# A Mamba block between two routed feed-forwards on one core: the next unit's transposes stand one third of a product sooner in TensorE's order

## The chip, the core and the metric

The kernel runs on one NeuronCore of a Trainium2 chip. The metric is the device time of one execution in microseconds. Before the change three runs took 2841.54, 2841.79 and 2851.29 us; the median is 2841.79 us.

## What is computed

4096 tokens (2 sequences of 2048) of 1024 features go through three residual stages:

```python
x = x + 0.5 * _L0_ffn_ref(_layernorm(x), A, B, W, bias)
x = x + _L0_attn_ref(_layernorm(x), W_xproj, W_dt, b_dt, A_log, D_param)
x = x + 0.5 * _L0_ffn_ref(_layernorm(x), A, B, W, bias)
```

The feed-forward projects each row on 64 experts of rank 16, keeps the four with the largest norm, and adds their low-rank update to a dense product:

```python
vecs = jnp.einsum('arh,bsh->bsar', A, x)
_, idx = jax.lax.top_k(jnp.linalg.norm(vecs, axis=-1), 4)
routes = jax.nn.one_hot(idx, 64).sum(-2) / 4
v = jnp.einsum('bsa,bsar->bsr', routes, vecs)
delta = jnp.einsum('bsa,ajr,bsr->bsj', routes, B, v)
base = jnp.einsum('bsh,jh->bsj', x, W) + bias
```

The middle stage is a selective scan with 16 states per feature: from a small projection come delta (a softplus), B and C; each state follows h = exp(delta A) h + delta B x, and y is the sum over the states of h C, plus x D.

## The kernel before, in words

**Units.** The 4096 tokens are 32 blocks of 128 rows. A block passes the first feed-forward as a unit of kind 1 and the second as a unit of kind 2, so there are 64 units, in an order that `plan` sets. The program of each engine is written out by hand as one `unit(l, a, b)` per unit: a is the present unit, l the one before, b the next. TensorE works on the base and routed products of a and, at the end, on the expert products of b.

**The scan** is cut into 256 groups of four (128 x 512) tiles. Each group is multiplied by B on POOL (`times_b`), decayed by exponentials on ACT (`decay`, line 855), scanned on DVE (line 1062), multiplied by C on POOL (`times_c`, line 459) and summed over the states on TensorE (`states`, line 651: four instructions, which the trace shows as eight). The groups are spread over units 5 to 57, four or five to a unit. The deltas come from a product on TensorE (`z`, line 638), a softplus on ACT (lines 814 to 829) and a product on DVE; they are written to delta_scratch and read back, broadcast over the states, by SP's queue.

**From a's choice to b's experts**, which is the part around the change. DVE sums the squares of the expert products (line 1010) and picks the four largest (`choose`), gathers the chosen vector and writes it to sel (`gather`), and SP's queue transposes it into uT. TensorE meanwhile runs a's base product (xT by wW), then a's routed product (uT by wB). Each product is made in two halves of 512 columns (nb 0 and 1) and each half in three thirds of eight matmuls 128x512: high part of the rows by high and low weights, k 0 to 3 (third 0) and k 4 to 7 (third 1), both line 491, and the low part of the rows by the high weights (third 2, line 495).

DVE takes the statistics of b's rows (`unit_stats`), ACT refines the inverse deviation in small steps (lines 740 to 754) and writes the normalised rows to xn (`normed`, line 764). TensorE transposes xn in eight 128x128 blocks (`norm_blocks`, line 483): the first four into pv, the other four into pt. The first call waits for xn:

```python
def norm_blocks(b, half):
    if half == 0:
        pe.wait_ge(s_xn, b.u + 1)
    if half == 0:
        pe.wait_ge(s_u, b.u * 2)
```

ACT copies each half to the high part of xT (`high`, line 769), DVE subtracts that to make the low part (`low_part`, line 1006). On both engines these two steps stand among decays and scans in a fixed order. After both high copies and the first low one TensorE may start the 48 matmuls of b's experts (`experts`, xT by wA into pv); its third third waits for the second low part. ACT squares the result (`squares`, line 777), and the next choice begins. In units of kind 1 ACT normalises a's rows a second time for the scan (`normed2`, line 787), ahead of the second call of `squares`.

All four engines and SP's queue execute in order. A wait holds back everything behind it on its engine, and semaphores are the only ties between engines.

Of the kernel before, what the change touches and what calls it, by code (L numbers as in the profile page):

```python
# [78 lines left out]
def build(nc, x, AT, BT, WT, bias, WxT, WdtT, b_dt, A_log, D_par, out):  # L79
# [38 lines left out]
    with ctx:  # L118
# [359 lines left out]
        def _(pe):  # L478
            pe.wait_ge(s_id, 3)

            def blocks(dst, src, sem_done, idt):
                for k in range(KB):
                    last = nc.tensor.transpose(dst[:, k * P:(k + 1) * P], src(k), idt)
                last.then_inc(sem_done, 1)

            def product(dst, lhs, w, nb, third, first, stop):

                if third < 2:
                    for k in range(third * KB, (third + 1) * KB):
                        for wb in range(2):  # L490
                            last = nc.tensor.matmul(dst, lhs[:, 0, k, :], w[:, wb, k, nb * HF:(nb + 1) * HF],  # L491
                                                    start=(first and k == 0 and wb == 0), stop=False)
                else:
                    for k in range(KD):
                        last = nc.tensor.matmul(dst, lhs[:, 1, k, :], w[:, 0, k, nb * HF:(nb + 1) * HF],  # L495
                                                start=False, stop=(stop and k == KD - 1))
                return last
# [6 lines that stand above are left out]
                blocks(ptn[half], lambda k: xn[:, (half * KB + k) * P:(half * KB + k + 1) * P], s_xT, idf[:, :])  # L504

            def y_blocks(b, half):
                if half == 0:
                    pe.wait_ge(s_ldy, b.v * 16 + 16)
                else:
                    pe.wait_ge(s_u, b.u * 2)  # L510
                blocks(pty[half], lambda k: auxy[:, half * KB + k, :], s_yT, idf[:, :])
# [50 lines left out]
            def base(a, nb, third):  # L562
                if a.u == 0:
                    if nb == 0 and third == 0:
                        first_base(a)
                    return
                if third == 0:
                    pe.wait_ge(s_res, max(a.u * 2 - 1 + nb, 0))
                    nc.tensor.matmul(po[:, nb, :], onesb[:, :], brow[:, nb * HF:(nb + 1) * HF], start=True, stop=False)
                product(po[:, nb, :], xT, wW, nb, third, False, False)  # L570

            def first_routed(a):

                pe.wait_ge(s_uc[0], 16)
                pe.wait_ge(s_uc[1], 16)
                for k in range(KD):
                    pe.wait_ge(s_hiB, k + 1)
                    for part in range(2):
                        for nb in range(2):
                            nc.tensor.matmul(po[:, nb, :], uT[:, part, k, :], wB[:, 0, k, nb * HF:(nb + 1) * HF],  # L580
                                             start=False, stop=False)
                for k in range(KD):
                    if k < KB:
                        pe.wait_ge(s_loB, k + 1)
                    else:
                        pe.wait_ge(s_loBp, k + 1 - KB)
                    for nb in range(2):
                        last = nc.tensor.matmul(po[:, nb, :], uT[:, 0, k, :], wB[:, 1, k, nb * HF:(nb + 1) * HF],
                                                start=False, stop=(k == KD - 1))
                        if k == KD - 1:  # L590
                            last.then_inc(s_out, 1)

            def routed(a, nb, third):
                if a.u == 0:
                    if nb == 0 and third == 0:
                        first_routed(a)
                    return
                if nb == 0 and third != 1:
                    pe.wait_ge(s_uc[third // 2], 16 * a.u + 16)
                last = product(po[:, nb, :], uT, wB, nb, third, False, True)  # L600
                if third == 2:
                    last.then_inc(s_out, 1)

            def scan_blocks(l, half):
                if half == 0:
                    pe.wait_ge(s_xn2, l.w + 1)
                else:
                    pe.wait_ge(s_nc, l.w * 2 + 1)
                blocks(pt, lambda k: xn[:, (half * KB + k) * P:(half * KB + k + 1) * P], s_nT, idf[:, :])
# [13 lines left out]
            def turn_products(l):  # L623

                pe.wait_ge(s_pk, l.w + 1)
                nc.tensor.transpose(pj[:, 2 * P:3 * P], pjs[:, 0:P], idf[:, :])
                nc.tensor.transpose(pj[0:NX - P, 3 * P:4 * P], pjs[:, P:NX], idf[:, :]).then_inc(s_pq, 1)

            def z(a, pos):
                if pos not in a.zs:  # L630
                    return
                t = a.zs[pos]
                q, k = t // KD, t % KD
                if k == 0:
                    pe.wait_ge(s_ldr, 16 * (q + 1))
                pe.wait_ge(s_gm, a.u + 1)
                pe.wait_ge(s_dc, t)
                nc.tensor.matmul(pz, wdt[:, k * P:(k + 1) * P], drT, start=True, stop=True).then_inc(s_z, 1)

            def states(a, n):  # L640

                G = slot_of(a, n)
                if G is None or G < 2 or G - 2 >= NGRP:
                    return
                G -= 2
                g = G % 4
                pe.wait_ge(s_cm, G + 1)
                if g == 0:
                    pe.wait_ge(s_y, G // 4)
                for s in range(4):  # L650
                    last = nc.tensor.matmul(py[32 * s:32 * s + 32, :], Em[:, :], Hr[:, G % NH, s, :],  # L651
                                            start=(g == 0), stop=(g == 3), tile_position=(0, 32 * s))
                last.then_inc(s_e, 1)

            def unit(l, a, b):
                late = l if l and l.kind == 1 else None
                y = b if b and b.kind == 2 else None
                base(a, 0, 0)
                if late:
                    scan_blocks(late, 0)  # L660
                base(a, 0, 1)
                states(a, 0)
                base(a, 0, 2)
                if late:
                    scan_blocks(late, 1)
                z(a, 0)
                base(a, 1, 0)
                if y:
                    if late:
                        pe.wait_ge(s_nc, late.w * 2 + 2)  # L670
                    y_blocks(y, 0)
                if y:
                    y_blocks(y, 1)
                base(a, 1, 1)
                base(a, 1, 2)
                states(a, 1)
                if late:
                    scan_products(a, late, y)
                if late:
                    pe.wait_ge(s_nc, late.w * 2 + 2)  # L680
                if y:
                    pe.wait_ge(s_ya, y.v * 2 + 2)
                routed(a, 0, 0)
                if late:
                    turn_products(late)
                routed(a, 0, 1)
                if late:
                    pe.wait_ge(s_pc, late.w + 1)
                routed(a, 0, 2)
                states(a, 2)  # L690
                routed(a, 1, 0)
                z(a, 1)
                routed(a, 1, 1)
                if b:
                    norm_blocks(b, 0)
                if b:
                    norm_blocks(b, 1)
                routed(a, 1, 2)
                states(a, 3)
                z(a, 2)  # L700
                if b:
                    experts(b, 0, 0)
                if b:
                    experts(b, 0, 1)
                if b:
                    experts(b, 0, 2)
                if b:
                    pe.wait_ge(s_dc, a.z_end)
                    experts(b, 1, 0)
                if b:  # L710
                    experts(b, 1, 1)
                if b:
                    experts(b, 1, 2)
                states(a, 4)
# [4 lines left out]
            for l, a in zip([None] + US, US):  # L719
                unit(l, a, a.after)  # L720
# [491 lines left out]
```

## Time and profile before

| | |
|---|---|
| median of the runs | 2841.79 us (2841.54 to 2851.29) |
| profiled execution: span | 2851.0 us |
| the run it is taken to be | 2851.29 us, the highest of the three |
| PE busy | 2604.9 us, 91% |
| POOL busy | 2347.1 us, 82% |
| DVE busy | 2189.6 us, 77% |
| ACT busy | 1448.4 us, 51% |
| PE weight loads | 1158.5 us, 41% |

The span is the time from the first to the last instruction of one profiled execution. A busy share is an average over the whole span: POOL works only while the scan runs, from about 300 to 2640 us, so its share there is much higher than the 82%. In rows of the trace "L483" is line 483 of the kernel; PE is TensorE, PEld its weight loads. A number in square brackets in a row is the idle time of the engine just before, with what ended it.

### The profile page before, as it was taken

The page shows a single profiled execution, that of the slowest core. Times are in us where ns is not written, and L with a number is a line of the kernel's source. Part 1 is how long each engine was busy: PE and PEld are TensorE (multiplying, and loading weights), DVE is VectorE, ACT ScalarE, POOL GpSimd, SP SyncE. Part 2 cuts the span into 40 slices and gives each one's busy share as a digit, 9 for nine tenths or more (in the row PEclk, how much of TensorE's full clock was granted, in tenths as well). Part 3 has the DMA queues.
Part 4 walks back from the last instruction along what each step waited for, and adds up shares of the span by engine and source line. Part 5 has one row for each costly group of instructions (what it writes and reads, how often), then busy time and mean ns, then how long its engine had stood idle before and what let it go on. Part 6 is the DMA issues. An engine that isn't in the chain of part 4 may idle for free.

```text
span 2851.0 us, 38123 instructions
## 1 busy us (share of the span) xinstructions
PE 2604.9 (91%) x13056; PEld 1158.5 (41%) x13120; DVE 2189.6 (77%) x2661; ACT 1448.4 (51%) x3075; POOL 2347.1 (82%) x703
## 2 busy tenths in 40 slices
PE   4998999999899999989999999999899989988999
PEld 1454444444333434334444343444334433433444
DVE  7434788788888878888888788888888888878533
ACT  5334565555555555545655465555555545454211
POOL 2103999899999999999899999999999999999300
PEclk8999999999999999999999999999999999999999
DMA  5125445554445444554454346444454455444221
GB/s 214 51 62 132 140 133 137 155 154 141 127 131 159 129 129 139 154 137 134 130 167 133 116 131 169 144 127 141 148 148 144 118 157 148 123 137 122 67 60 52
DMA packets 309368, 373.40 MB, mean 131 GB/s; under 512 B 148147, under 2 KB 224051, under 8 KB 309174
## 3 DMA queue, kind: packets, MB, share of 16 engines
q1 hardware_dynamic: 292278, 337.40, 40.7%
q10 hardware_dynamic: 16896, 33.56, 4.0%
q8 instruction: 104, 1.70, 0.2%
q14 instruction: 90, 0.74, 0.1%
HBM read 234.05 MB, written 103.29 MB: 118 GB/s over the span
## 4 chain that ended last, share of the span: by engine, by line
PE 22%; DVE 18%; POOL 10%; DMA 8%; issue 7%; DVEq 5%; ACT 4%; ACTq 1%; SPq 1%; POOLq 0%
DVE mreg L1062 9%; PE pv L491 7%; POOL mreg L459 5%; PE po L491 5%; PE pv L495 3%; POOL mreg L451 3%; DMA delta_scratch<-mreg 3%; PE po L495 3%; DMA mreg<-xnT_scratch 2%; PE py L651 2%; ACT pA L855 1%; POOL mreg L446 1%; DMA uT<-sel 1%; DVE pv L1029 1%; DVE sel L1026 1%
## 5 line engine op out<-in xcount | busy, mean ns | idle before, releaser
L459 POOL TENSOR_TENSOR mreg<-mreg 128x2048 f32<-128x2048 f32 x256 | 1161.1, 4536 | 20.9 <-ACT hst L844 20.7
L1062 DVE TENSOR_TENSOR_SCAN mreg<-pA,hst,mreg 128x512 f32<-128x512 f32 x768 | 940.1, 1267 | 75.5 <-ACT hst L844 45.5
L451 POOL TENSOR_TENSOR mreg<-mreg 128x1024 f32<-128x1024 f32 x340 | 795.8, 2365 | 234.9 <-DMA mreg<-delta_scratch 231.9
L855 ACT ACTIVATE pA<-mreg,nA 128x512 f32<-128x512 f32 x1024 | 696.7, 684 | 467.2 <-DVE mreg L1062 412.9
L491 PE MATMUL po<-wB,uT 128*128 128x512 f16 x2016 | 476.7, 386 | 30.3 <-DMA uT<-sel 16.9
L491 PE MATMUL pv<-wA,xT 128*128 128x512 f16 x2016 | 462.4, 383 | 39.6 <-ACT xT L769 30.5
L491 PE MATMUL po<-wW,xT 128*128 128x512 f16 x2016 | 467.0, 380 | 8.0 <-issue 7.0
L446 POOL TENSOR_TENSOR mreg<-mreg 128x2048 f32<-128x2048 f32 x86 | 390.7, 4544 | 1.6 <-issue 1.6
L1062 DVE TENSOR_TENSOR_SCAN mreg<-pA,cst,mreg 128x512 f32<-128x512 f32 x256 | 313.4, 1267 | 30.4 <-ACT hst L844 20.7
L491 PEld LDWEIGHTS pv<-wA,xT 128*128 128x128 f16 x2016 | 194.0, 99 | 320.6 <-ACT xT L769 76.6
L491 PEld LDWEIGHTS po<-wB,uT 128*128 128x128 f16 x2016 | 192.7, 99 | 321.9 <-issue 94.2
L651 PE MATMUL py<-mreg,Em 128*32 128x512 f32 x2048 | 272.9, 605 | 50.2 <-POOL mreg L459 40.7
L491 PEld LDWEIGHTS po<-wW,xT 128*128 128x128 f16 x2016 | 197.6, 98 | 225.6 <-issue 13.7
L1010 DVE TENSOR_REDUCE n<-sel 128x32 f32<-128x512 f32 x128 | 86.6, 677 | 250.0 <-ACT sel L777 249.9
L495 PE MATMUL pv<-wA,xT 128*128 128x512 f16 x1008 | 243.2, 385 | 27.0 <-DVE xT L1006 27.0
L495 PE MATMUL po<-wB,uT 128*128 128x512 f16 x1008 | 243.2, 385 | 0.0
L495 PE MATMUL po<-wW,xT 128*128 128x512 f16 x1008 | 240.1, 381 | 0.0
L495 PEld LDWEIGHTS pv<-wA,xT 128*128 128x128 f16 x1008 | 98.6, 99 | 150.9 <-issue 36.4
L1042 DVE SCALAR_TENSOR_TENSOR xin<-po,sc,xin 128x512 f32<-128x512 f32 x128 | 92.2, 721 | 85.8 <-PE po L495 82.4
L495 PEld LDWEIGHTS po<-wW,xT 128*128 128x128 f16 x1008 | 94.5, 98 | 151.6 <-issue 45.7
L777 ACT ACTIVATE sel<-pv 128x512 f32<-128x512 f32 x128 | 75.4, 590 | 152.5 <-PE pv L495 148.0
L495 PEld LDWEIGHTS po<-wB,uT 128*128 128x128 f16 x1008 | 100.2, 99 | 108.6 <-issue 6.0
(132 smaller groups left out, 2346.9 us busy)
## 6 DMA issues: line engine op xcount, KB each, us to landing
mreg<-delta_scratch SPq DMA_DIRECT2D x256, 512.0 KB, 5.6
delta_scratch<-mreg ACTq DMA_DIRECT2D x128, 256.0 KB
xin<-x SPq DMA_DIRECT2D x32, 512.0 KB, 4.5
x_scratch<-xin SPq DMA_DIRECT2D x32, 512.0 KB, 7.2
xnT_scratch<-auxs SPq DMA_DIRECT2D x32, 512.0 KB, 2.9
mreg<-xnT_scratch SPq DMA_DIRECT2D x64, 256.0 KB, 6.4
mreg<-bc_scratch SPq DMA_DIRECT2D x64, 256.0 KB, 5.5
yT_scratch<-mreg SPq DMA_DIRECT2D x64, 256.0 KB, 2.4
```

The lines of the kernel that those rows point to most:

```text
L446: pool.tensor_tensor(Hr[:, G % NH, :, :], u, b.broadcast_to([P, 4, CT]), ALU.mult).then_inc(s_bm, 2)
L451: pool.tensor_tensor(Hr[:, G % NH, 2 * h:2 * h + 2, :], u, b.broadcast_to([P, 2, CT]), ALU.mult).then_inc(s_bm, 1)
L459: pool.tensor_tensor(h, h, Cr[:, g, :].unsqueeze(1).broadcast_to([P, 4, CT]), ALU.mult).then_inc(s_cm, 1)
L491: last = nc.tensor.matmul(dst, lhs[:, 0, k, :], w[:, wb, k, nb * HF:(nb + 1) * HF], start=(first and k == 0 and wb == 0), stop=False)
L495: last = nc.tensor.matmul(dst, lhs[:, 1, k, :], w[:, 0, k, nb * HF:(nb + 1) * HF], start=False, stop=(stop and k == KD - 1))
L651: last = nc.tensor.matmul(py[32 * s:32 * s + 32, :], Em[:, :], Hr[:, G % NH, s, :], start=(g == 0), stop=(g == 3), tile_position=(0, 32 * s))
L777: nc.scalar.activation(sel[:, nb * HF:(nb + 1) * HF], pv[:, nb, :], ACT.Square).then_inc(s_sq, 1)
L855: nc.scalar.activation(pA[:, i % 2, :], Dr[:, 2 * (n % NPR) + i % 2, :], ACT.Exp, scale=nA[:, c:c + 1]).then_inc(s_dA, 1)
L1010: V.tensor_reduce(n2[:, nb * NE // 2:(nb + 1) * NE // 2], sel3[:, nb * NE // 2:(nb + 1) * NE // 2, :], AX.X, ALU.add)
L1026: V.tensor_tensor(ranked, pv[:, :, :].rearrange("p b (a r) -> p r (b a)", r=R16), mask[:, :].unsqueeze(1).broadcast_to([P, R16, NE]), ALU. ...
L1042: V.scalar_tensor_tensor(dst, po[:, nb, :], sc[:, 3:4], dst, ALU.mult, ALU.add).then_inc(s_res, 1)
L1062: V.tensor_tensor_scan(h, pA[:, i % 2, :], h, before, ALU.mult, ALU.add).then_inc(s_sc, 1)
```

## The change

In TensorE's `unit`, the two calls of `norm_blocks` for the next unit move ahead of the call `routed(a, 1, 1)`. The eight matmuls of that call now stand behind the transposes, together with the eight of `routed(a, 1, 2)`.

```diff
@@ -690,11 +690,11 @@
                 states(a, 2)
                 routed(a, 1, 0)
                 z(a, 1)
+                if b:
+                    norm_blocks(b, 0)
+                if b:
+                    norm_blocks(b, 1)
                 routed(a, 1, 1)
-                if b:
-                    norm_blocks(b, 0)
-                if b:
-                    norm_blocks(b, 1)
                 routed(a, 1, 2)
                 states(a, 3)
                 z(a, 2)
```

TensorE's order in a scan unit, from the state products `states(a, 2)` (py) over the second half of the routed product (po<-wB,uT) and the transposes (pv and pt from idf,xn) to the expert products (pv<-wA,xT); before:

```order
L651 MATMUL py<-mreg,Em 32x512 x4
L491 MATMUL po<-wB,uT 128x512 x16
L483 MATMUL pv<-idf,xn 128x128 x4
L483 MATMUL pt<-idf,xn 128x128 x4
L495 MATMUL po<-wB,uT 128x512 x8
L651 MATMUL py<-mreg,Em 32x512 x4
L491 MATMUL pv<-wA,xT 128x512 x16
```

The same place after the change:

```order
L651 MATMUL py<-mreg,Em 32x512 x4
L491 MATMUL po<-wB,uT 128x512 x8
L483 MATMUL pv<-idf,xn 128x128 x4
L483 MATMUL pt<-idf,xn 128x128 x4
L491 MATMUL po<-wB,uT 128x512 x8
L495 MATMUL po<-wB,uT 128x512 x8
L651 MATMUL py<-mreg,Em 32x512 x4
L491 MATMUL pv<-wA,xT 128x512 x16
```

The sixteen matmuls of line 491 are split: eight stand ahead of the transposes as before, eight behind. The other engines' orders and the DMA queues are unchanged, as is the first unit, whose routed product is written in another form.

## Rows read from the trace of the kernel before

**Rows 1.** Busy time by stretch: us, then each engine's busy time (instructions).

```profile
core 0: us, PE busy (x) PEld busy (x) DVE busy (x) ACT busy (x) POOL busy (x), PEclk, DMA share, GB/s
700.00:2640.00 1940.00, 1780.25 (x8980) 773.50 (x9022) 1608.76 (x1902) 1049.51 (x2200) 1876.51 (x552) 0.98 0.48 139
2700.00:2851.00 151.00, 145.94 (x696) 68.69 (x697) 50.77 (x84) 23.25 (x60) 0.00 (x0) 1.00 0.20 56
```

**Rows 2.** Waits from 300 to 2640 us: engine line <- releaser: us, times, longest.

```profile
DVE n L1010 <- ACT sel L777: 151.3, 60, 4.5
...
POOL mreg L451 <- DMA mreg<-delta_scratch: 52.5, 21, 6.4
...
PE pv L491 <- ACT xT L769: 29.2, 23, 3.1
PE pv L483 <- ACT xn L764: 27.9, 23, 2.7
```

**Rows 3.** Chain that ended last, its first piece: start us, us, what.

```profile
709.71 0.04 issue
```

**Rows 4.** The same chain, pieces around the experts' start in three units.

```profile
1060.99 0.70 DVE xT L1006
...
1332.33 0.52 ACT xT L769
...
1332.88 0.70 DVE xT L1006
...
1333.72 3.61 PE pv L491 x16
...
1344.28 0.61 ACT sel L777
...
2374.67 0.70 DVE xT L1006
```

**Rows 5.** The same chain, the eight matmuls ahead of the transposes.

```profile
1465.16 1.73 PE po L491 x8
```

**Rows 6.** Timeline of unit 60: start us, us, engine, line, operation.

```profile
2703.84 1.24 ACT L764 ACTIVATE xn<-xin,ln_nm,ln_r 128x1024 f32<-128x1024 f32 x1
...
2711.05 0.60 PE L483 MATMUL pv<-idf,xn 128*128 128x128 f32 x4
```

**Rows 7.** Timeline around 1465 us.

```profile
1464.63 1.24 ACT L764 ACTIVATE xn<-xin,ln_nm,ln_r 128x1024 f32<-128x1024 f32 x1
...
1466.72 0.60 PE L483 MATMUL pv<-idf,xn 128*128 128x128 f32 x4
```

**Rows 8.** Timeline around 1330 us.

```profile
1328.31 1.24 ACT L764 ACTIVATE xn<-xin,ln_nm,ln_r 128x1024 f32<-128x1024 f32 x1
...
1329.61 0.66 PE L483 MATMUL pv<-idf,xn 128*128 128x128 f32 x4 [0.63 <-ACT xn L764]
...
1330.54 1.89 PE L495 MATMUL po<-wB,uT 128*128 128x512 f16 x8
...
1332.36 1.06 PE L651 MATMUL py<-mreg,Em 128*32 128x512 f32 x8
...
1333.72 1.46 PE L491 MATMUL pv<-wA,xT 128*128 128x512 f16 x6 [0.29 <-DVE xT L1006]
```

**Rows 9.** The chain again, pieces of the passages from xn to the matmuls.

```profile
1368.90 1.25 ACT xn L764
...
1371.64 3.06 PE po L495 x8
...
2594.94 1.25 ACT xn L764
```

**Rows 10.** Timeline around 875 us.

```profile
874.45 1.24 ACT L764 ACTIVATE xn<-xin,ln_nm,ln_r 128x1024 f32<-128x1024 f32 x1
...
876.20 0.60 PE L483 MATMUL pv<-idf,xn 128*128 128x128 f32 x4
```

**Rows 11.** Timeline of TensorE at 1370 us.

```profile
1370.20 0.66 PE L483 MATMUL pv<-idf,xn 128*128 128x128 f32 x4 [2.37 <-ACT xn L764]
```

**Rows 12.** Busy time by stretch, 1368 to 1376 us (PEclk follows POOL).

```profile
1368.00:1376.00 8.00, 5.80 (x26) 2.57 (x27) 7.03 (x9) 6.07 (x12) 8.00 (x4) 0.79 0.55 167
```

More of the change, by code:

```diff
@@ L692, in unit @@
                 z(a, 1)
-                routed(a, 1, 1)
                 if b:
@@ L697, in unit @@
                     norm_blocks(b, 1)
+                routed(a, 1, 1)
                 routed(a, 1, 2)
```

## The prediction, made before the changed kernel was run

> **What bounds the kernel now.** I read the time by stretches first. In the scan stretch from 700 to 2640 us POOL works 1876.5 of 1940 us (97%), TensorE 1780.3 (92%) and DVE 1608.8 (83%); in the last 151 us POOL does nothing and TensorE works 145.9 us [rows 1]. So the ends are TensorE's alone, and in the middle three engines are close to each other. The table of waits says that none of them is a bound that hides the others. POOL stops 21 times for rows that come back from delta_scratch, 52.5 us in all. DVE stops 60 times for the squares of the expert products, 151.3 us. TensorE stops 23 times for the normalised rows (27.9 us) and 23 times for the ACT copies of xT (29.2 us) [rows 2]. The last two waits are the ones on either side of what the change moves.
>
> Then I read the chain of waits, since in such a balance it alone says what a microsecond is worth. It reaches back to 709.71 us [rows 3] and no further; of what lies ahead of that I have only the other views. It changes engines many times in each unit. The piece at 1332 us shows the part that matters: DVE makes the low half of xT, TensorE runs the 48 expert products after it, ACT squares them from 1344.28 us [rows 4], DVE sums and chooses, and only then come the scans of the next unit. When the experts start late there, all that follows is late.
>
> **What the change does at one passage.** The eight matmuls that change places with the transposes take 1.73 us [rows 5]. Nothing is added or removed: the matmuls and the transposes are the same, no DMA is issued sooner or later by its own queue, and ACT, DVE, POOL and SP keep their order. So the direct cost is nothing, and all depends on when the rows (xn) are ready. Three cases occur in the trace.
>
> (a) TensorE comes late. In the last units xn begins at 2703.84 us and takes 1.24, and the transposes run at 2711.05, 5.97 us after its end [rows 6]. They go 1.73 us sooner, TensorE waits for nothing before or after, and the sum stays: 0. The units ahead of the scans are of this kind too.
>
> (b) TensorE comes a little late. At 1464.63 + 1.24 = 1465.87 us the rows are ready and the transposes start at 1466.72 [rows 7], 0.85 later. They can go only 0.80 us sooner (about 0.05 passes between the end of xn and the first transpose where TensorE waits for it [rows 8]), so what stands behind is 1.73 - 0.80 = 0.93 us later. In ten or so units of this kind the experts start later than TensorE is free, by 0.9 us or more, since ACT's second copy stands behind a softplus. The 0.93 is taken up there, and I cost it at 0; if ACT were ready, it would cost 0.93 each.
>
> (c) TensorE comes first. At 1328.31 us xn begins; TensorE has waited 0.63 us when it transposes at 1329.61; eight matmuls follow at 1330.54, the eight state products at 1332.36, then 0.29 us of waiting, and the experts start at 1333.72 [rows 8]. Now TensorE waits for xn 1.73 us longer, the transposes start when they did, and sixteen matmuls stand behind them. It is ready for the experts 1.73 us later than before, 0.29 of which was a wait for xT. The experts start 1.73 - 0.29 = 1.44 us later. The added cover hides nothing that was open beyond these 0.29 us.
>
> By the timeline some 30 of the 53 scan units are of kind (c), but only those on the chain count. In several units of the first feed-forward, whose rows are normalised a second time, the chain goes through ACT's and DVE's own work, and the experts have time to spare. **The passages on the chain** are these:
> - low half of xT to experts: six times, the first at 1060.99 us and the last at 2374.67 [rows 4], each with the same wait of 0.29 or 0.30 before the experts: 6 x 1.44 = 8.6 us.
> - xn to transposes to matmuls to experts without a further wait: three times, the first at 1368.90 us and the last at 2594.94 [rows 9]: 3 x 1.73 = 5.2 us.
> - at 876.20 us TensorE comes 0.51 us after the end of xn (874.45 + 1.24) [rows 10] and there is no wait before the experts: 1.73 - 0.46 = 1.3 us.
> - the passage at 1466.72 us [rows 7], where POOL takes over from the state products behind the eight matmuls: 0.9 us.
>
> The sum is 16.0 us for 1931 us of scan units on the chain (709.7 to 2640). The scan units ahead of it, from about 300 to 710 us, show the same kinds of passage; an estimate in proportion is 16.0 x 410 / 1931 = 3.4 us. In all **+19.4 us**. The profiled execution has a span of 2851.0 us and lies at 2851.29 us, the highest of the three runs (their median is 2841.79). 2851.3 + 19.4 = 2870.7, a ratio of 1.0068, and on the median 2861.1: I forecast **2861 us**.
>
> The bounds. Below: the chain has near ties that I can't see, other executions are up to 10 us shorter and may follow another chain, and POOL's 97% may take up part of it: 0. Above: every one of 53 units late by 1.73 is 92 us, less the 29.2 us of waiting before the experts [rows 2], 63 us. I stay near the sum, since it is counted passage by passage on a chain without slack and nothing on that chain gets shorter.
>
> **The clock.** At the passage of 1368.90 us TensorE waited 2.37 us for xn [rows 11], and in the 8 us from 1368 the granted clock is 0.79 [rows 12], so a part ran at 1.2 GHz instead of 2.4. From the first transpose (1370.20) to the end of the eight matmuls (1371.64 + 3.06) it took 4.50 us [rows 9, 11], against 2.75 at full clock (1329.61 to 1332.36) [rows 8]: 1.75 us more. The change lengthens the wait ahead of the transposes by up to 1.73 us in kind (c) and shortens the one behind. I leave this out of the sum, since most waits of kind (c) become about 2 us long, shorter than the one of rows 11, and no row says what such a wait does. The Trainium skill (TensorE: Matmul & The Clock Gate, section "Why this matters for your kernels") advises against idle gaps between bursts of matmuls, because the clock falls to half; by that rule more passages would start at half clock after the change, and the sum would be that of rival 2, below.
>
> **Rivals.**
> 1. *POOL hides it.* POOL is busy 97% of the scan stretch, and the eight-matmul delays fall into DVE's and TensorE's slack while POOL goes on. The time stays at 2842. The Trainium skill (Perfetto Trace Analysis, section "Identifying the Most-Contended Engine") has the engine of highest occupancy as the one to optimise; read strictly, a delay on TensorE would then not count. Against it: POOL stops 21 times for the delta rows [rows 2], which come from a chain that starts with TensorE in the same unit. Chance 0.23.
> 2. *Half clock.* By the timeline 8 further passages of kind (c) get a wait about as long as that of rows 11 or longer; if each begins at half clock, at 1.75 us, that is 14 us on top, 2875 us. For it speaks the one clear case [rows 11, 12]. Against it: equally long waits just before the experts become shorter. Chance 0.20.
> 3. *Faster.* If the copies to xT were held by the transposes, transposing sooner would start the experts sooner and remove their waits for xT: at most 29.2 us [rows 2], 2841.8 - 29.2 = 2813 us. It decides in kinds (a) and (b), wherever the first copy starts at the end of the transposes. In kind (c) the transposes can't go sooner. And even where they can, in scan units ACT is busy with decays: the copy at 1332.33 [rows 4] began 2 us after its four transposes, which had started at 1329.61 and taken 0.66 [rows 8]. Chance 0.07.
>
> **How the numbers follow.** My own case has 0.50 and spans 2848 to 2872. A measurement of this kernel can tell about 0.5% from no change, which is 14.2 us: slower begins at 2856. Some of my own case (0.08) lies under it, so slower is 0.42 + 0.20 = 0.62, plus 0.01 from late switches of the chain: 0.63. Within 0.5%: 0.23 + 0.08 = 0.31, less that 0.01 and with 0.01 of the third rival: 0.31. Faster 0.06. The range from 2843 to 2880 leaves out the third rival, about half of the first and the upper tail.
>
> **What would show it.** In the changed profile TensorE's wait for xn (23 times, 27.9 us) should grow to 60 to 90 us over 30 units or more, its wait for the xT copies should fall from 29.2 to under 15, and in kind (c) the experts should start 5.6 us after the end of xn instead of 4.2. DVE's wait for the squares should grow by 10 to 40 us, and POOL's busy time in the scan stretch should stay while the stretch gets longer. I am wrong if the wait for xn grows but POOL's idle time does not, or if the copies to xT start sooner and the experts with them.

## The result, and the profile after

| | before | after |
|---|---|---|
| median of the runs | 2845.3 us (2841.54 to 2851.29) | 2883.95 us (2881.77 to 2886.15) |
| profiled execution, span | 2851.0 us | 2881.9 us |
| PE busy | 2604.9 us | 2622.8 us |
| POOL busy | 2347.1 us | 2346.8 us |
| share of PE in the chain that ended last | 22% | 27% |

A further run of the kernel before moved its median from 2841.79 to 2845.3 us. Its profiled execution is the slowest of its runs, so the two spans are only 31 us apart. The ratio is **1.0131**, with a 95% interval from 1.0119 to 1.0143: the change costs about 37 us. The forecast had the sign and the places right, but 19.4 us and a range that ended at 2880.

The waits from 300 to 2670 us, the same scan units as in [rows 2] (engine, line, releaser: us in total, times, longest):

```profile
DVE n L1010 <- ACT sel L777: 170.5, 60, 5.6
PE pv L483 <- ACT xn L764: 106.1, 50, 4.4
...
POOL mreg L451 <- DMA mreg<-delta_scratch: 69.6, 22, 6.7
...
PE pv L491 <- ACT xT L769: 3.8, 8, 1.0
```

TensorE's wait for the normalised rows grew from 27.9 to 106.1 us and from 23 to 50 times. Its wait for xT went from 29.2 to 3.8 us. DVE waits 19 us longer for the squares, and POOL 17 us longer for the delta rows. The other waits of POOL over the same units, first before, then after:

```profile
POOL mreg L459 <- ACT hst L844: 19.1, 8, 3.2
POOL mreg L451 <- PE py L651: 3.0, 4, 1.5
POOL mreg L446 <- issue: 1.6, 2, 1.4
```

```profile
POOL mreg L459 <- ACT hst L844: 20.4, 8, 3.3
POOL mreg L446 <- issue: 8.2, 5, 2.3
POOL mreg L451 <- PE py L651: 8.2, 5, 3.4
```

With the delta rows that is 76.2 us before and 106.4 after. POOL's work is the same (2347.1 and 2346.8 us), so its 30 us more of waiting are the 31 us between the two spans. The late experts reach the time as idle time of POOL, 17 us of it at the delta rows.

Busy time by stretch (columns as in [rows 1]), the scan units and the end:

```profile
700.00:2670.00 1970.00, 1796.96 (x8970) 780.63 (x9012) 1609.27 (x1900) 1048.68 (x2201) 1875.53 (x551) 0.97 0.47 136
2730.00:2881.00 151.00, 146.93 (x702) 69.26 (x703) 51.67 (x85) 23.23 (x60) 0.00 (x0) 1.00 0.20 56
```

Against [rows 1] the scan stretch takes 30 us more for the same work of POOL (1875.5 us and 1876.5), and the end is unchanged. The granted clock of the scan stretch is 0.97 instead of 0.98.

The chain that ended last, at the passage that answers to [rows 8]:

```profile
1331.87 1.25 ACT xn L764
...
1333.17 0.66 PE pv L483 x4
1333.82 0.44 PE pt L483 x4
1334.26 1.73 PE po L491 x8
1335.98 1.73 PE po L495 x8
1337.71 1.00 PE py L651 x8
1338.71 3.56 PE pv L491 x16
...
1349.21 0.61 ACT sel L777
```

This is kind (c) as the prediction drew it. The rows end at 1333.12 us, the transposes follow at once, then sixteen matmuls and the state products, and the experts start at 1338.71 without a wait: 5.6 us after the end of xn instead of 4.2. The chain now runs from xn through TensorE. In the traced part of before, from 709.7 us, it did so three times; after, in a traced part that is shorter (from 1011.1 us), it does so 23 times, 19 of them in the 26 units that the experiments single out below, and four in others. The first and the last:

```profile
1054.57 1.25 ACT xn L764
...
2667.52 1.25 ACT xn L764
```

The next passage shows the other part of the loss. The timeline of TensorE, and the busy time with the granted clock (third number from the end):

```profile
1375.13 1.11 PE L483 MATMUL pv<-idf,xn 128*128 128x128 f32 x4 [4.09 <-ACT xn L764]
...
1376.89 3.58 PE L491 MATMUL po<-wB,uT 128*128 128x512 f16 x8
...
1382.13 1.06 PE L651 MATMUL py<-mreg,Em 128*32 128x512 f32 x8
1383.12 1.25 PE L491 MATMUL pv<-wA,xT 128*128 128x512 f16 x5
```

```profile
1374.00:1382.00 8.00, 6.87 (x24) 3.60 (x24) 7.05 (x9) 5.33 (x9) 8.00 (x4) 0.61 0.64 208
```

The same passage of before waited 2.37 us [rows 11] at a clock of 0.79 [rows 12]. Now TensorE waits 4.09 us and then works at 1.2 GHz for longer: the granted clock over 8 us is 0.61, the first eight matmuls take 3.58 us, against 1.89 for eight at full clock [rows 8], and the experts start 8.0 us after the end of xn. By the clock records of the traces TensorE was at the lower level for 68 us (17 stretches) between 280 and 2700 us before, and for 109 us (26 stretches) after.

### The profile page after: what moved, and what is told of

Same layout as the page of the kernel before. It is cut to its first block, busy times and chain, and to the rows that moved or that the text cites. A ratio compares the mean times of both kernels' runs of the same rounds, so it can differ in the third digit from the quotient of the medians.

```text
span 2881.9 us, 38123 instructions
## 1 busy us (share of the span) xinstructions
PE 2622.8 (91%) x13056; PEld 1165.8 (40%) x13120; DVE 2191.3 (76%) x2661; ACT 1447.6 (50%) x3075; POOL 2346.8 (81%) x703
## 4 chain that ended last, share of the span: by engine, by line
PE 27%; DVE 12%; DMA 7%; POOL 4%; issue 4%; DVEq 4%; ACT 4%; SPq 1%; ACTq 1%; POOLq 0%
PE pv L491 7%; PE po L491 7%; DVE mreg L1062 6%; PE pv L495 4%; PE po L495 4%; DMA delta_scratch<-mreg 2%; DMA xin<-x_scratch 2%; PE py L651 2%; DMA mreg<-xnT_scratch 2%; POOL mreg L459 2%; POOL mreg L451 2%; DVEq L984 1%; ACT xn L764 1%; PE pv L620 1%; POOL mreg L446 1%
## 5 line engine op out<-in xcount | busy, mean ns | idle before, releaser
L491 PE MATMUL po<-wB,uT 128*128 128x512 f16 x2016 | 498.3, 395 | 25.8 <-DVE xin L992 15.3
L491 PEld LDWEIGHTS po<-wB,uT 128*128 128x128 f16 x2016 | 197.0, 101 | 305.3 <-issue 94.7
L495 PE MATMUL po<-wB,uT 128*128 128x512 f16 x1008 | 239.6, 381 | 0.0
L483 PE MATMUL pv<-idf,xn 128*128 128x128 f32 x256 | 45.7, 306 | 117.3 <-ACT xn L764 117.3
```

## The experiments

Theory W: the cost comes from the wait for the normalised rows, which stands eight matmuls sooner, in the units where TensorE comes first; it holds back what follows and lets the clock fall. The change itself is the first row of this table, and the two columns on the right are worked out from each kernel's own trace: the mean time from the end of xn to the first expert matmul over the 26 scan units without a delta product at position 1 (`1 not in a.zs`), and the time at the lower clock from 280 to 2700 us.

| kernel | ratio to before (95%) | experts after xn | lower clock |
|---|---|---|---|
| the change | 1.0131 (1.0119 to 1.0143) | 6.28 us | 109 us |
| before | 1 | 4.51 | 68 |
| e1 wait alone | 1.0117 (1.0099 to 1.0134) | 6.31 | 116 |
| e2 units with a delta product | 0.9991 (0.9982 to 1.0001) | 4.51 | 51 |
| e3 units without | 1.0130 (1.0110 to 1.0150) | 6.20 | 99 |
| e4 change and 8 filling matmuls | 1.0082 (1.0064 to 1.0100) | 5.67 | 82 |
| e5 before and 4 filling matmuls | 0.9999 (0.9989 to 1.0008) | 4.58 | 44 |
| e6 transposes later | 0.9996 (0.9986 to 1.0006) | 4.42 | 61 |
| e7 kind 1 alone | 1.0049 (1.0033 to 1.0065) | 5.46 | 72 |
| e8 kind 2 alone | 1.0092 (1.0075 to 1.0109) | 5.44 | 89 |
| e9 half the way | 1.0049 (1.0030 to 1.0069) | 5.41 | 82 |
| e10 copies sooner | 0.9993 (0.9982 to 1.0003) | 4.36 | 61 |
| e11 copies sooner, transposes later | 0.9981 (0.9971 to 0.9990) | 3.77 | 55 |

**The wait alone, e1.** The transposes stay; one wait is added.

```diff
+                if b:
+                    pe.wait_ge(s_xn, b.u + 1)
                 routed(a, 1, 1)
                 if b:
                     norm_blocks(b, 0)
```

> The transposes stay where they were; only TensorE's wait for the normalised rows stands eight matmuls sooner. Theory W (the cost is the earlier wait, and what the longer stop does to TensorE's clock): as slow as the change, 1.011 to 1.015 of the time before. Rival T (the cost comes from the transposes themselves standing sooner, by the copies of xT or the banks of PSUM): as before the change, 0.999 to 1.002.

It measured 1.0117, as the change. TensorE's waits from 300 to 2670 us show the same stop, now ahead of the eight matmuls, whose first line is 491:

```profile
PE po L491 <- ACT xn L766: 100.2, 51, 4.4
```

So the place of the transposes plays no part that these runs can tell (the two intervals overlap). What costs is that TensorE may not do eight matmuls that it could do before xn is there.

**Where it costs, e2 and e3.** The transposes stand sooner only in units that meet a condition, `1 in a.zs` in e2 and `1 not in a.zs` in e3.

```diff
-                routed(a, 1, 1)
-                if b:
+                sooner = 1 in a.zs
+                if b and sooner:
                     norm_blocks(b, 0)
-                if b:
                     norm_blocks(b, 1)
+                routed(a, 1, 1)
+                if b and not sooner:
+                    norm_blocks(b, 0)
+                    norm_blocks(b, 1)
                 routed(a, 1, 2)
```

> The change in the 27 units alone that have a delta product at position 1, where TensorE comes to the transposes late or ACT holds the copies. Theory W: 0.999 to 1.003. Rival U (every unit pays alike): 1.006 to 1.007.

> The change in the other units alone (26 in the scan and those around it), where TensorE comes to the transposes first. Theory W: 1.010 to 1.014, nearly all of the loss. Rival U: 1.006 to 1.007.

The 27 units with a delta product at position 1 cost nothing (0.9991), the others all of it (1.0130). By the trace of before, most of the 27 are of kind (b), and in seven TensorE comes first but the experts wait for ACT. Over the 27 the experts start 5.99 us after the end of xn in before and 6.09 in e2. So kind (b) was rightly put at zero. Kind (a), the units at the two ends, lies in e3, and the unchanged end above speaks for its zero. In e2 TensorE does wait for xn more often from 300 to 2670 us,

```profile
PE pv L483 <- ACT xn L767: 52.5, 42, 3.3
...
PE pv L491 <- ACT xT L772: 6.0, 9, 1.3
```

but 23 us of its wait for xT are gone in exchange: there ACT's second copy, behind the softplus, sets the experts' start in either order.

**The clock, e4.** The change, with work that fills the wait in the 26 units.

```diff
                 if half == 0:
-                    pe.wait_ge(s_xn, b.u + 1)
-                if half == 0:
                     pe.wait_ge(s_u, b.u * 2)
+                if half == 0 and b.u > SCAN0 and 1 not in US[b.u - 1].zs and b.u <= SCAN1:
+                    for _ in range(8):
+                        nc.tensor.matmul(pt[:, :], onesb[:, :], brow[:, 0:HF], start=True, stop=True)
+                if half == 0:
+                    pe.wait_ge(s_xn, b.u + 1)
```

> The change, and in the 26 scan units without a delta product at position 1 eight matmuls that compute nothing ahead of the wait for the normalised rows, so that TensorE works there as long as it did before. The order and its delay behind the transposes stay. If half of the loss is the clock: 1.004 to 1.008 of the time before, and the stretches at half clock go back to about 20. If the clock has no part in it and only more passages were on the chain than were counted: 1.012 to 1.018.

It measured 1.0082. The filling matmuls add work and change no order behind the transposes, and yet 0.49% of the time, 14 us, came back (about 8 to 20 by the two intervals). The passage of e4 that answers to the one at 1375 us above (TensorE's timeline, then busy time with the clock):

```profile
1372.20 0.66 PE L483 MATMUL pv<-idf,xn 128*128 128x128 f32 x4 [2.36 <-ACT xn L767]
...
1376.68 1.06 PE L654 MATMUL py<-mreg,Em 128*32 128x512 f32 x8
1377.68 3.63 PE L491 MATMUL pv<-wA,xT 128*128 128x512 f16 x16
```

```profile
1370.00:1378.00 8.00, 5.79 (x34) 2.76 (x35) 7.05 (x9) 6.07 (x12) 8.00 (x4) 1.00 0.57 180
```

TensorE stops for 2.36 us instead of 4.09, the clock stays at 1.00, and the experts start 5.5 us after the end of xn (1370.91 + 1.24 = 1372.15), not 8.0. The length of one stop doesn't settle it alone: before the change the stop here was 2.37 us and the clock fell (0.79). Over the 26 units the mean is 5.67 instead of 6.28 us. The time at the lower clock didn't go back to 68 us but to 82: the units with a delta product have the sooner wait and no filling, and two of the 26 still start their experts 7.1 us after xn. So by the medians the clock costs about 14 us of the 37. An estimate of its most is 14 us plus half of the 14 us that are left at the lower level, 21 us; the interval of the 14 us comes on top.

**Filling the wait of before, e5.** The filling of e4, with four matmuls instead of eight, in the kernel before.

> The kernel before, with four matmuls that compute nothing (0.9 us) ahead of the wait for the normalised rows in the 26 scan units without a delta product at position 1. Where TensorE waits there by more than 0.9 us the work is free and the clock may stay up; elsewhere it costs up to 0.9 us. Clock theory: 0.997 to 1.002, with less time at half clock than the 68 us of before. If the length of the stop has no part in the clock: 1.003 to 1.008, since about half of the 26 units pay.

It measured 0.9999. The time at the lower clock fell from 68 to 44 us, which would be worth up to 12 us if TensorE worked through all of it, but the run is no faster. The experts start no sooner on average (4.58 us), and that mean hides two things. In the four of the 26 units that began at the lower clock before (xn ends there at 1100, 1370, 2456 and 2596 us) they start 4.2 us after xn instead of 5.4 to 5.5. In seven others they start 0.2 to 0.6 us later, since the filling is added to what TensorE has to do. In two (2134 and 2631 us) TensorE comes only 3.6 to 4.0 us after the end of xn, held up mainly further ahead, and the experts start 2.2 to 2.3 us later. So e5 gives no price of the clock by itself: what full clock brought was lost elsewhere.

**Later instead of sooner, e6.** In the 26 units the transposes stand after all sixteen matmuls.

```diff
+                later = SCAN0 <= a.u < SCAN1 and 1 not in a.zs
                 routed(a, 1, 1)
-                if b:
+                if b and not later:
                     norm_blocks(b, 0)
-                if b:
                     norm_blocks(b, 1)
                 routed(a, 1, 2)
+                if b and later:
+                    norm_blocks(b, 0)
+                    norm_blocks(b, 1)
```

> The opposite move in the same 26 scan units: the transposes after all sixteen matmuls. Theory W (TensorE is held by the rows, and ACT and DVE by their own queues): TensorE's stop gets 1.73 us shorter, the experts start as before or up to 0.3 us later: 0.992 to 0.999. Rival C (the eight matmuls behind the transposes are needed as cover for the copies to xT): the experts start 1 to 1.7 us later, 1.005 to 1.012.

It measured 0.9996: neither. Rival C falls, since eight matmuls of cover can go without loss; the gain that theory W put at 0.1% or more isn't there either. Timeline of e6 around the passage at 1330 us:

```profile
1320.09 1.24 ACT L767 ACTIVATE xn<-xin,ln_nm,ln_r 128x1024 f32<-128x1024 f32 x1
...
1322.34 0.60 PE L483 MATMUL pv<-idf,xn 128*128 128x128 f32 x4
...
1323.42 0.69 ACT L858 ACTIVATE pA<-mreg,nA 128x512 f32<-128x512 f32 x1 [0.80 <-DVE mreg L1065]
...
1324.05 0.58 ACT L772 ACTIVATE xT<-pv 128x512 f16<-128x512 f32 x1
...
1324.66 0.69 DVE L1009 TENSOR_TENSOR xT<-pv,xT 128x512 f16<-128x512 f32 x1 [0.16 <-ACT xT L772]
...
1325.50 2.75 PE L491 MATMUL pv<-wA,xT 128*128 128x512 f16 x12 [0.39 <-DVE xT L1009]
```

The transposes come 1.0 us after the end of xn, and the experts still 4.2 us after it, because ACT's first copy stands behind three decays, the last of which (line 858 here) waited 0.80 us for a scan of DVE.

**By the kind of unit, e7 and e8.** The change in the 12 units of kind 1 and in the 14 of kind 2 among the 26, with a condition as in e2.

> The change in the 12 scan units of kind 1 without a delta product at position 1 alone. By the chain of before, ACT's second normalisation leaves the experts time in most of these: 1.001 to 1.005. If every unit without such a product pays alike: 12/26 of the loss, 1.006.

> The change in the 14 scan units of kind 2 without a delta product at position 1 alone. By the chain of before, most of the loss: 1.007 to 1.012. If every unit pays alike: 14/26 of the loss, 1.007.

They measured 1.0049 and 1.0092. The two add up to the whole (1.0141 against 1.0131, within the intervals). Per unit that is 1.2 us for kind 1 and 1.9 us for kind 2. Kind 2 pays more, as the chain of before had it, though the delay is about the same: by the table the experts of the 26 units start 25 us later in sum in e7 and 24 in e8, and 14 and 26 us of that reach the time. So the second normalisation of kind 1 takes up part of a delay, about four tenths here, but not all, and kind 1 is at the upper end of what I expected.

**Half the way, e9.** The product's second third is cut in two, four matmuls ahead of the transposes and four behind, in all units. The last argument of `product`, which the cut below doesn't define, picks the k of the third.

```diff
-                routed(a, 1, 1)
+                if a.u:
+                    product(po[:, 1, :], uT, wB, 1, 1, False, True, (0, 2))
                 if b:
                     norm_blocks(b, 0)
-                if b:
                     norm_blocks(b, 1)
+                if a.u:
+                    product(po[:, 1, :], uT, wB, 1, 1, False, True, (2, 4))
                 routed(a, 1, 2)
```

> Half the change in all units: the transposes stand four matmuls sooner, with 12 behind them. In the 26 scan units without a delta product at position 1 TensorE is ready for the experts 0.86 us later, 0.3 of which was a wait: the experts start 4.7 us after the end of xn instead of 4.2. Theory W, order alone: 26 x 0.56 x 0.8 = 12 us, 1.004; with some more stretches at half clock up to 1.007. If a cost jumps in with the first matmul moved: 1.010 or more. If the last four moved carry it all: 1.000 to 1.002.

It measured 1.0049 (1.0030 to 1.0069), 37% of the loss for half the way. The cost grows with the number of matmuls held back; half of the loss (1.0066) lies inside the interval, so the run doesn't show a growth faster than in proportion. Where the clock stays up the experts mostly start 4.7 us after xn, as expected. In ten of the 26 units they start 6.0 us or more after it, so the mean is 5.41 and the delay half of the full one (0.90 of 1.77 us).

**ACT's and DVE's own order, e10 and e11.** In the 26 units ACT's copies of xT stand ahead of decay 14, and DVE's first low part ahead of scan 13; e11 has the transposes of e6 as well.

```diff
                 magnitudes(a, 1)
-                decays(14, 15)
+                early = SCAN0 <= a.u < SCAN1 and 1 not in a.zs
+                if not early:
+                    decays(14, 15)
                 if b:
                     high(b, 0)
...
                     high(b, 1)
+                if early:
+                    decays(14, 15)
...
-                scans(10, 14)
+                early = SCAN0 <= a.u < SCAN1 and 1 not in a.zs
+                scans(10, 13 if early else 14)
                 if b:
                     low_part(b, 0)
+                if early:
+                    scans(13, 14)
```

> TensorE's order of before. In the 26 scan units ACT's two copies of xT stand one decay sooner and DVE's first low part one scan sooner, so that they end before TensorE is through with the matmuls behind the transposes. The 0.3 us of waiting goes: 26 x 0.3 x 0.8 = 6 us, 0.998. If a decay or scan that stands later holds POOL: 1.000 to 1.004.

> The same on ACT and DVE, and the transposes after all sixteen matmuls in these 26 units. Theory W: the experts can start about 3.3 us after the end of xn instead of 4.2, 26 x 0.9 x 0.8 = 19 us less, 0.993, and less time at half clock; at least 0.997. If DVE or POOL bounds these units and not TensorE: 0.999 to 1.002.

They measured 0.9993 (0.9982 to 1.0003) and 0.9981 (0.9971 to 0.9990). Both gains are smaller than I expected: 0.998 for e10, 0.993 and at least 0.997 for e11. e11 is the fastest version of the study. Its experts start 0.74 us sooner than before on average over the 26 units, 19 us in sum, but the run gains 5. Two waits of e11 from 300 to 2640 us bear on this:

```profile
PE py L651 <- POOL mreg L459: 58.6, 52, 2.7
...
POOL mreg L451 <- DMA mreg<-delta_scratch: 39.3, 17, 5.6
```

POOL waits 13 us less for the delta rows than in [rows 2]. TensorE, which is ahead now, stops 52 times for POOL's products with C, 58.6 us; in the kernel before it was

```profile
PE py L651 <- POOL mreg L459: 39.5, 37, 2.8
```

The 19 us won at the experts stand again as 19 us more of waiting at the state products. A part of POOL's 13 us belongs to the runs and not to the change: the traces are of e11's fastest run and of the slowest of before, and e2, whose profiled run took 2840.97 us, waits 49.1 us for the delta rows and 38.3 us for POOL's products. That meeting POOL is what eats the gain is a reading. e11 also sets a decay and a scan later in each of these units, and no run gives the cost of that by itself.

## Why the prediction was wrong in size

**What bounds the kernel, and kind (a), (b), (c): right.** The end didn't change (151 us in both profiles), nor did what lies ahead of the scan units (the rows of the first of them end at 281.3 and 280.7 us), e2 shows the units with a delta product, those of kind (b) among them, at 0.9991, and kind (c) starts its experts 5.5 to 5.6 us after xn wherever the clock stays up. The signs named for the waits came true, the first beyond its bound: 106 us against 60 to 90. POOL's idle time grew with them, by 30 us.

**The step that failed first: "I leave this out of the sum, since most waits of kind (c) become about 2 us long".** It was the clock. The time at the lower level grew by 41 us, and e4 shows that about 14 of the 37 us hang on it. The forecast priced the mechanism (1.75 us for a passage, 14 us for eight passages, 2875 us with chance 0.20) and then put it at nothing. That the price for eight passages equals e4's 14 us is partly luck: by the trace of after, ten of the 26 passages have their experts about 7.0 us or more after xn instead of 5.5, later by 1.5 to 2.9 us each. The reason given, that most waits become about 2 us long, was right for most but not for all: eight of the 26 stops ahead of the transposes became 3.5 us or longer, and seven of these eight are among the ten. Nor was the case of rows 11 alone: in the trace of before six of the 26 passages stopped for 2.4 to 2.7 us, and in four of them the clock fell. A passage that already waited 2.37 us and ran at 0.79 of the clock was one to which the change added 1.73 us of waiting; it should have been taken as the pattern for its like. The rule of the Trainium skill cited there (TensorE: Matmul & The Clock Gate, section "Why this matters for your kernels"), that idle gaps between bursts lower the clock, agrees with this trace: 4.09 us of waiting, then 0.61.

**The second: "but only those on the chain count", eleven passages for 16.0 us.** The order, as e4 measures it with what is left of the clock in it, costs 0.82%, 23 us, against 19.4 in the sum; by its interval it is 18 to 28 us, so the size of this miss is not clear of noise. What the runs do show is that the count was made of the wrong things. It took the chain of before as fixed. After the change the chain goes from xn to TensorE 23 times instead of three, since passages that had little to spare became the longest way. e7 shows it for kind 1: two of the eleven passages were of that kind, and its 12 units, whose spare time I trusted, lose 14 us together, the clock's part included. When every unit of a kind is delayed, the sum over one chain is nearer to a lower bound, and it was used as the middle. (Two slips in the working move nothing: the stretch from 709.7 to 2640 is 1930 us long, and 2841.79 + 19.4 is 2861.2.)

Another way to count comes out nearer. The experts of the 26 units start 1.77 us later on average (6.28 against 4.51), 46 us in sum, and 37 us arrive in the time, four fifths. The same working gives seven to eight tenths in e1, e3 and e4 as well, six in e9 and e7, and all of it in e8. So it differs by kind of unit, and four fifths is a mean of this kernel. **The bound "below: 0"** and rival 1, that POOL at 97% hides the delays, have no support: e1, e3, e4, e7, e8 and e9 all lose, and POOL itself waits 30 us longer after the change.

The rival "faster" is excluded by the change itself and by e2: on average transposing sooner starts the experts sooner in neither. The upper bound of 63 us held, and the range, 2843 to 2880, ended 4 us too low: it took the half-clock rival as the edge and left no room for both misses together.

What stays open is the exact split between order and clock, and why stops of nearly equal length (2.37 and 2.52 us in before) are followed by the lower clock in one unit and not in another. A filling that keeps TensorE busy in all 53 units without holding back anything wasn't found, and none was tried there, because where TensorE comes late a filling itself delays the experts.

## What to carry to other kernels

A wait placed ahead of work that doesn't need it costs that work's time whenever the engine arrives first, and on TensorE it can also cost the clock of what follows (here 0.61 over 8 us after a stop of 4.09 us); look in the trace for stops that are already long and price the change there at the lower clock. When many near-equal passages are delayed alike, the chain of before gives too little: count the delay of every passage of the kind, and take most of it (six tenths to all here, by kind of unit). A longer cover behind a transfer or copy is worth only the wait that stands there now, here 0.3 us.

## What the runs showed that I had not expected

Delays and gains weren't symmetric. In this balance four fifths of a delay of the experts reached the time (46 us, 37 measured), but only about a quarter of an advance (e11: 19 us, 5 measured, 3 to 8 by the interval). That the next engine, POOL here, is met at once fits the waits of e11 and isn't shown by a run of its own. And less time at the lower clock needn't show in the time: e5 had 24 us less at 1.2 GHz than before, 1.3 us sooner experts in four units, later ones in nine, and the same time.
